# Two copies of each row of C in DRAM in place of five, and four 32-partition loads in place of one

## The reference

```python
zxbcdt = x @ in_proj_w.T           # z, xv, Bm, Cm, dt_in
dt = softplus(dt_in @ dt_proj_w.T + dt_proj_b)
A = -exp(A_log)
dA = exp(dt[..., None] * A)        # 1024 channels x 16 states
dtx = (dt * x_full).reshape(b, l, GC, D_INNER // GC)
dBx = (dtx[..., :, None] * Bg[..., None, :]).reshape(b, l, D_INNER, D_STATE)
def step(h, inp):
    h = dA_i * h + dBx_i
    y = einsum('bgn,bgcn->bgc', C_i, h.reshape(b, GC, D_INNER // GC, D_STATE))
y = (y + D_skip * x_full) * silu(z)
return y @ out_proj_w.T
```

## Time and profile before

| what | value |
|---|---|
| median of 3 runs | 679.99 us (679.35 to 681.1) |
| the profiled execution: time | 679.04 us |
| the profiled execution: span from the first to the last instruction | 677.1 us |
| busy: PE, DVE, ACT, POOL | 632.5, 425.6, 345.3, 429.3 us |
| mean granted clock of TensorE | 0.977 |
| DMA | 163.51 MB in 49165 packets, mean 241 GB/s; 145.24 MB read from HBM, 17.69 MB written |
| loads of C (L383) | 64 transfers: 32 of 580 KB, 32 of 700 KB |
| stores of C (L371) | 16 transfers: 8 of 725 KB, 8 of 875 KB |

### The profile page before, as it was taken

How to read it: one execution, slowest core, us unless ns; L and a number is a source line. 1 busy time by engine, 2 the same in 40 slices (tenths; PEclk the granted TensorE clock), 3 DMA queues, 4 the chain that set the end, 5 groups by cost and what they waited for, 6 DMA issues and landing times.

```text
span 677.1 us, 8630 instructions
## 1 busy us (share of the span) xinstructions
PE 632.5 (93%) x2846; PEld 506.2 (75%) x2846; DVE 425.6 (63%) x660; ACT 345.3 (51%) x658; POOL 429.3 (63%) x244
## 2 busy tenths in 40 slices
PE   4969997799999889999979999999999999999998
PEld 3637674466665667777757777766999998999998
DVE  4088895899887889889897988861332232332132
ACT  4359989248999364333246333321543443543441
POOL 0276773537777899997877978744455464455561
PEclk9979997899999899999989999999999999999999
DMA  8799997379999969998876989643444344233421
GB/s 337 263 358 345 317 301 259 133 230 369 318 355 348 391 259 340 413 366 317 324 258 218 340 323 314 223 124 99 151 139 142 124 155 126 63 125 131 149 67 44
DMA packets 49165, 163.51 MB, mean 241 GB/s; under 512 B 4320, under 2 KB 18528, under 8 KB 48480
## 3 DMA queue, kind: packets, MB, share of 16 engines
q1 hardware_dynamic: 49120, 162.95, 69.2%
HBM read 145.24 MB, written 17.69 MB: 241 GB/s over the span
## 4 chain that ended last, share of the span: by engine, by line
PE 79%; DVE 9%; ACT 6%; issue 3%; DMA 2%; POOL 1%; SPq 0%; DVEq 0%; ACTq 0%
PE work L990 57%; PE da L990 15%; PE work L1000 6%; DVE da L781 4%; DVE hs L792 2%; ACT da L551 1%; ACT L528 1%; DMA bb<-b_rows 1%; DMA c_rows<-c_rows 1%; DMA sm<-small 1%; DVE a L847 0%; ACT L668 0%; ACT L551 0%; POOL hs L453 0%; DVE sq L864 0%
## 5 line engine op out<-in xcount | busy, mean ns | idle before, releaser
L781 DVE TENSOR_TENSOR_SCAN da<-da,hs 128x290 f32<-128x290 f32 (+1 forms) x256 | 198.2, 817 | 41.6 <-POOL hs L453 20.9
L453 POOL TENSOR_TENSOR hs<-dtx,bb 128x1160 f32<-128x1160 f32 (+1 forms) x64 | 171.2, 2677 | 62.5 <-PE work L1000 50.4
L551 ACT ACTIVATE da<-dt,a_neg 128x261 f32<-128x261 f32 (+1 forms) x256 | 118.4, 495 | 131.0 <-DVE hs L792 130.5
L432 POOL TENSOR_TENSOR ws<-wraw,ws 128x1024 fp32r<-128x1024 f32 x40 | 101.5, 2538 | 92.7 <-ACT ws L559 92.7
L990 PE MATMUL work<-sq,wraw 128*128 128x290 f32 x512 | 126.0, 407 | 1.3 <-DVE sq L880 0.8
L990 PEld LDWEIGHTS work<-sq,wraw 128*128 128x128 f32 x512 | 96.4, 189 | 30.8 <-issue 1.7
L990 PE MATMUL work<-hn,win 128*128 128x290 f32 (+1 forms) x336 | 102.6, 453 | 17.5 <-DVE hn L855 8.0
L792 DVE TENSOR_TENSOR hs<-da,cb 128x580 f32<-128x580 f32 (+1 forms) x128 | 105.2, 822 | 11.2 <-DMA cb<-c_rows 4.5
L990 PEld LDWEIGHTS work<-hn,win 128*128 128x128 f32 x336 | 65.2, 198 | 50.1 <-issue 25.3
L559 ACT CAST ws<-wraw 128x1024 fp32r<-128x1024 f32 x48 | 50.3, 1048 | 70.7 <-PE da L990 34.3
L990 PE MATMUL work<-hn,ws 128*128 128x350 f32 x480 | 79.2, 323 | 1.6 <-DVE hn L951 1.6
(11 more groups left out here) (99 smaller groups left out, 649.0 us busy)
## 6 DMA issues: line engine op xcount, KB each, us to landing
wraw<-w_stream SPq DMA_DIRECT2D x104, 512.0 KB, 3.6
bb<-b_rows SPq DMA_DIRECT2D x32, 700.0 KB, 6.7
cb<-c_rows SPq DMA_DIRECT2D x32, 700.0 KB, 4.7
bb<-b_rows SPq DMA_DIRECT2D x32, 580.0 KB, 8.5
cb<-c_rows SPq DMA_DIRECT2D x32, 580.0 KB, 6.6
c_rows<-c_rows SPq DMA_DIRECT2D x8, 875.0 KB, 11.6
c_rows<-c_rows SPq DMA_DIRECT2D x8, 725.0 KB, 6.9
win<-w_in SPq DMA_DIRECT2D x4, 1024.0 KB, 14.0
```

What stands on the lines that cost most here:

```text
L432: nc.gpsimd.tensor_tensor(ws[:, k % NW, 1, :], wraw[:, split_loads[k] % NRAW, :], ws[:, k % NW, 0, :].bitcast(F32), ALU.subtract).then_inc ...
L453: nc.gpsimd.tensor_tensor(hs[:, u % NH, 0:NQ * n].rearrange("p (n t) -> p n t", t=n), dtx[:, t % 2, 0:n].unsqueeze(1).to_broadcast([P, NQ, ...
L551: last = nc.scalar.activation(dst, src, ACT.Exp, scale=a_neg[:, j:j + 1])
L781: nc.vector.tensor_tensor_scan(da[:, k % ND, 0:w], da[:, k % ND, 0:w], hs[:, u % NH, p * w:(p + 1) * w], 0.0, ALU.mult, ALU.add).then_inc( ...
```

## The change

The rows of C are written twice (256 rows, 64 blocks) in place of 5 times. Block 8q + 31 lies within 64 for each q, so the 32 blocks that a unit needs stand one after the other. `load_c` issues four transfers in a row, one for each 32 partitions, and all four read these same 32 blocks. DVE waits for all four: 64 counts in place of 16. B, the buffers, the order of the queue and all computation stay.

```diff
--- before.py
+++ after.py
@@ -63,6 +63,8 @@
 
 REPL = P // 8
 COPIES = (REPL + NQ - 1 + NQ - 1) // NQ
+
+C_COPIES = 2
 SPLITS = 4 * (HH + KD)
 LOADS = KD + SPLITS
 
@@ -190,7 +192,7 @@
     load_of = {s: i for i, s in enumerate(readers)}
     split_loads = [i for i, s in enumerate(readers) if s[0] != "out" and s[1] == NCH - 1]
     split_of = {readers[i]: k for k, i in enumerate(split_loads)}
-    c_dram = [nc.dram_tensor(f"c_rows{c}", (KI, COPIES * P, TS[c]), F32, kind="Internal").ap() for c in range(NCH)]
+    c_dram = [nc.dram_tensor(f"c_rows{c}", (KI, C_COPIES * P, TS[c]), F32, kind="Internal").ap() for c in range(NCH)]
     b_dram = [nc.dram_tensor(f"b_rows{c}", (COPIES * XB, TS[c]), F32, kind="Internal").ap() for c in range(NCH)]
 
     with ExitStack() as ctx:
@@ -369,7 +371,7 @@
             def store_c(c, m):
                 freed(sp, ("in_c", c, m))
                 sp.dma_start(c_dram[c][m].rearrange("(k p) t -> p k t", p=P),
-                             c_rows[:, m % 2, 0:TS[c]].unsqueeze(1).to_broadcast([P, COPIES, TS[c]])).then_inc(
+                             c_rows[:, m % 2, 0:TS[c]].unsqueeze(1).to_broadcast([P, C_COPIES, TS[c]])).then_inc(
                                  c_stored[m % 2], 16)
 
             def load_c(u):
@@ -379,8 +381,9 @@
                     sp.wait_ge(c_times, products_through(u - NC))
                 if q == 0:
                     sp.wait_ge(c_stored[m % 2], 16 * ((KI * c + m) // 2 + 1))
-                src = c_dram[c][m].rearrange("(o i n) t -> o i (n t)", i=4, n=NQ)[2 * q:2 * q + 2 * REPL]
-                sp.dma_start(cb[:, u % NC, 0:w], src).then_inc(c_loaded[u % NC], 16)
+                rows = c_dram[c][m].rearrange("(i n) t -> i (n t)", n=NQ)[8 * q:8 * q + 32]
+                for r in range(P // 32):
+                    sp.dma_start(cb[32 * r:32 * r + 32, u % NC, 0:w], rows).then_inc(c_loaded[u % NC], 16)
 
             def load_w(i):
                 if i >= len(readers):
@@ -787,7 +790,7 @@
                 w = GS[c] * TS[c]
                 here = slice(2 * j * w, 2 * (j + 1) * w)
                 if j == 0:
-                    dve.wait_ge(c_loaded[u % NC], 16 * (u // NC + 1))
+                    dve.wait_ge(c_loaded[u % NC], 16 * P // 32 * (u // NC + 1))
                 dve.wait_ge(scan_done, k + 2)
                 nc.vector.tensor_tensor(hs[:, u % NH, here].rearrange("p (i w) -> p i w", w=w), da[:, k % ND:k % ND + 2, 0:w],
                                         cb[:, u % NC, here].rearrange("p (i w) -> p i w", w=w), ALU.mult).then_inc(c_times, 1)
```

## The result

The changed kernel is slower by 8%: 741.95 us (median of 4 runs, 732.54 to 756.15) against 680.55; ratio 1.081, interval 1.077 to 1.0851. A second series beside other kernels gave 734.52 against 681.6, ratio 1.0769 (1.0741 to 1.0797).

A forecast was written before the change was run, and what follows sets the result against it. The prediction took TensorE's chain as the bound, transfers close behind. With loads of C at factor 2, stages overrun by 7 us at 408 GB/s to 26 at 370; the middle, 16, onto 679.99 gave 696 us, range 677 to 708.

The forecast's parts named there:

- The bound: Whole kernel: the chain names mostly TensorE; the 16 DMA engines, 92 to 98% busy in long stretches, come close behind.
- The signs that the prediction named: 130 to 219 and 244 to 343 us: share above 0.9, GB/s under 316 and 339; `cb` landing 8 us, waits over 10.
- Stores: 16 stores of C write 2 copies, not 5: 1.1 or 1.3 us less each, 19 us of queue time.
- loads that run at line rate: Rival for loads of C: factor 1, so saved stores count; 678.2 us, 675.5 to 680, chance 0.27.
- Issue on SP: Loads of C on SP's queue: four instructions for one, 69 us added in all, covered on average by SP's waits.
- SP held back by a full queue: Rival on SP's queue: four transfers fill it sooner, weights and B come late; 11 us, 691 us, chance 0.05.
- Loads, transfer: All 64 loads of C, 103 us at 408 GB/s: writing 32 partitions per transfer slows them by factor 1 to 4.
- The factor 2: Loads of C take twice as long, the middle of 1 and 4 as a ratio; 687 to 707 us, chance 0.46.
- the sum built on it: Seven stages from 26 to 449 us: bytes less saved stores, C's loads counted again; overrun 7 to 26 us, middle 16.
- the seam: Start of the second chunk's recurrence, where DVE's wait for a load of C ended at 217.93 us before the change.
- The range: Whole kernel: 677 to 708 us, leaving out about a quarter of the line-rate case and the case towards factor 4.
- The row of 268 GB/s: Two-microsecond stretch of the profile before the change: what a full queue delivers while stores are under way.

The follow-up runs named there:

- measured with one transfer: Against the changed kernel, a load of C is one transfer reading each of 32 blocks into four neighbouring partitions, values misplaced; 675.78 us against 679.86 before the change, ratio 0.9939.
- the mixture: Separate kernel without computation: second-chunk loads of B, C and weights in a never-empty queue; 288 GB/s with C in four neighbours, 408 with C whole.
- The kernel with moved channels: Against the kernel before: channels moved, two copies of C, whole loads with right values, B in four copies read into eight neighbours; 740.01 us, ratio 1.0833.
- B of eight alone: Kernel with two copies and one transfer per load of C, altered so a load of B reads 16 rows into eight neighbours each; ratio 1.0452, 709 to 714 us.

## Why the prediction was wrong

*The bound.* Right: the transfers were the resource next in line, and they became the bound, through DVE's and POOL's waits early and TensorE's waits for weights from the second chunk on. The signs that the prediction named for it came: between 130 and 343 us the DMA share stayed above 0.9 with fewer GB/s, DVE's waits for `cb` went from 4.5 to 37.9 us, and in the second chunk a quarter load landed after 17.3 us (median).

*Stores.* Right in sign, with the measured size at the far end of the range: −1.8 us (0 to −4.4) forecast for loads that run at line rate, −4.1 us (−2.2 to −6.0) measured with one transfer.

*Issue on SP.* Forecast 1.08 us more per load; measured 1.38 (issues after the first take 0.42 us, not 0.32: 3 × 0.46). That is hidden, as forecast: four transfers of every fourth partition cost 0.3% in all, even with slower issues. SP held back by a full queue was seen (four issues took 5.43 us at 205.85 us) but was not the cause: the kernel with every fourth partition has as many transfers, with issues of 0.59 us (median).

*Loads, transfer: the step that failed.* The factor 2 itself covers what a load of C costs alone: 406 / 232 = 1.75. What failed is the sum built on it, which counted the bytes of the loads of C once more and left B and the weights at 370 to 408 GB/s. In a full queue of mixed loads, a load of C costs 2.27 us more than its 1.76 us, 2.3 times as much; in the kernel it is more still. From 250 to 450 us DVE made 44 products, so 22 loads of C in 200 us, 9.1 us each, at a mean of 252.5 GB/s: 2.30 MB. Without C's 0.717 MB, 1.58 MB would take 4.3 us at 370 GB/s. That leaves 4.8 us for a load of C that takes 1.94 at that rate, a factor of 2.5 if all of the loss is counted as C's.

The trace's packets show that it is not C's alone. From 250 to 450 us a packet of weights (4,096 bytes) took 187 ns on average before the change and 260 after it, and 190 in the kernel with every fourth partition. Packets of B and C (5,600 bytes) took 240 ns before and 366 after; three quarters of them took over 340, and only half of them are C's (a unit loads as much of B as of C), so B is slowed too.

The prediction's own sum shows the size of the step. The stages from 219 to 449 us hold 9.0 + 33.6 + 8.0 + 20.1 − 1.1 = 69.6 MB and 30 loads of C, 21.5 MB, in 230 us. At 370 GB/s they come to 232 us with the factor 1.75, to 246 with 2, to 264 with 2.3 and to 275 with 2.5; 45.9 us more than 230 were measured, that is 276. So the loads' own slowness (1.75) explains 2 us, what they cost in a mixture (2.3) explains 34, and the last 12 have no experiment of their own. Read with the measured rate it is simpler: 69.6 MB at 252.5 GB/s need 276 us. That is accounting, since the rate comes from these same stretches, but it is the sum to make as soon as a rate of the mixture is at hand.

Up to the seam the forecast (an overrun between 0 and 10 us) held: 7.3. A factor of 2.5 at 370 GB/s would have given 30 us there, so the cost of a load of C is not one factor for both chunks; why it is lower in the first chunk isn't shown.

*The range.* Its upper part ended at 707 since 370 GB/s, the rate of the queue before, was taken as the worst rate for the traffic that was not changed. The row of 268 GB/s shows how slowly busy engines can go; it was read as a matter of stores and not used as a bound for the rest.

*The page's rule.* The Trainium skill, "SBUF — State Buffer", "Can I just issue two DMAs to hit both halves?" has it that the only way to reach all 16 ports is one transfer spanning all 128 partitions. The runs add that this is not enough: one transfer of 128 partitions from 16 rows ran at 231 GB/s. Nor must a transfer fill them all: those of every second partition ran at 390 and of every fourth at 391 among whole ones. These reach across all 128, and whether the page means them by spanning it doesn't say.

*What stays open.* That engines meet at a common port of SBUF would fit these rows, but it is a guess: the rows show rates, shares and packet times, not ports, nor how the rows of a transfer are dealt out to the engines. Why a load of C costs 2.5 times as much in the kernel and 2.3 times in the mixture wasn't separated; weights' packets took 260 ns in the one and 213 in the other, but before the change they had also taken more in the kernel (187 against 160). The kernel with moved channels is some 26 us slower than the one with B of eight alone; its late start explains about 10 of them (first product with C at 48.5 us in place of 38.9), the rest wasn't looked into. A version with two copies, the right values and whole loads of both C and B wasn't found: with C in neighbours, B needs each row four times side by side in DRAM, and the stores for that were not tried.

## What to carry to other kernels

When a transfer is cut up, ask which partitions each piece writes, and not only how many bytes or transfers there are: pieces of 32 neighbours run at 0.57 of the whole rate, pieces of every fourth partition at 0.95 or more of it when SP keeps ahead of the engines (391 and 396 GB/s among other loads). In a full queue a slow kind of transfer is paid by the others too, so rate the whole stage's bytes with the rate of the mixture (here 250 GB/s in place of 370) and not only the changed transfers with a factor. A DMA share near 1 with GB/s far below the best slice is the sign of it.

## What the runs showed of the hardware that was not expected

- Loads of 32 neighbouring partitions slow other loads in the same queue: a unit loses 2.27 us where the quarters alone cost 1.32, and 0.64 of it is lost by packets of weights (213 ns in place of 160).
- The order of four such transfers matters: 253 against 232 GB/s alone, 329 against 288 in the mixture, 1.0391 against 1.0769 in the kernel.
- One row read into 2 or 4 neighbouring partitions costs 1 or 2% (404 and 399 GB/s against 408), into 8 it costs 43% (231).
- Stores of B whose DRAM side begins with a dimension of 4 took 10.40 us to land, in a queue of eight with 145 KB each. The Trainium skill, page "DMA: Bandwidth & Descriptors", section "Why a DMA increments its semaphore by 16 and not by 1", says that the slowest dimension limits the number of engines, which by its rule would be 4 here; this row is in keeping with it, and no run here varied that dimension alone.
